# Message table of an edge network in six parts whose first turns are computed on the chip

## The chip, the cores and the metric

One core of one Trainium2 chip runs the kernel. The metric is the device time of one execution in microseconds (us). TensorE (PE), VectorE (DVE), ScalarE (ACT), GpSimd (POOL) and SyncE (SP) run side by side and meet at semaphores.

## The reference

The graph has 12,500 nodes with 128 features and 412,500 edges: 200,000 random pairs in both directions and a self loop for each node, sorted by destination. Two layers follow each other.

```python
# layer 0
agg = segment_sum(edge_weight[:, None] * x[src], dst)
x = layernorm(x + relu((x + agg) @ W1 + b1) @ W2 + b2)
# layer 1
h1 = x @ lin1_w.T
c = 0.5 * (cos(edge_weight * pi / 10) + 1)
s = softplus(edge_attr @ nn_w1.T + nn_b1) - log(2)
msg = (softplus(s @ nn_w2.T + nn_b2) - log(2)) * c[:, None] * h1[dst]
agg = segment_sum(msg, src)
out = layernorm(x + (h1 + agg) @ lin2_w.T + lin2_b)
```

Layer 0 sums over the destination, by which the edges are sorted. Layer 1 reads its rows by the destination and sums over the source, by which they are not sorted.

## The kernel before

The edges are cut into T = 403 tiles of 1024 edges (SUB = 8 columns of 128). The program has five stages: a setup, the edges of layer 0, the nodes of layer 0, the edges of layer 1 (`layer1_edges`) and the nodes of layer 1.

**Edges of layer 0.** For each tile POOL gathers eight times 128 rows of x (L432, tile `xg`), from indices that ACT copies (`gidx`, L411). DVE builds one-hot columns (`onehot`, L563), and PE multiplies the two (L475). The tiles xg, gidx and onehot have one buffer each: POOL waits for the multiplication that last read its row tile, ACT for the gathers that last read its indices. Beside this, PE computes the first layer of the edge network (L481, into two banks), ACT its softplus (L395 to L399), and DVE finishes it in `hidden(t, 0)` and `hidden(t, 1)` (L506); SP stores it (L363).

**Sorting for layer 1.** The same stage works out where each message will go. The sources fall into NB = 100 buckets of 128 nodes. The tiles are split into PARTS = 4 parts of 101, 101, 101 and 100 tiles. In each part every bucket owns whole blocks of 512 rows (floor(count/512) + 1 of them) in a table in DRAM (`sorted_messages`, two tables, each of two parts). DVE counts the sources of each bucket with `count_bucket` (L699), an operation over all columns of the part. For part 0 that is done in the setup, 100 times over 808 columns. For the part after the current one it is done once in each tile, between `hidden(t, 0)` and `hidden(t, 1)` (L589 to L592). At the start of a part `plan_part` turns the counts into row numbers, into `ends` (the last block of each bucket) and into the lists `slot_node` and `slot_row`, with small DVE operations and small matmuls (L438 to L449, L510 to L535). SP clears with zeros the last block of each bucket, one clear in each tile (L376), and two blocks at the end of each part (L382), since only the last block is partly filled.

**Edges of layer 1.** For each tile DVE makes the messages (L1248, L1257), and POOL scatters them with eight indirect DMAs to their rows (L1204). The blocks are summed in turns of TURN = 3: SP loads 3 blocks (792 KB, L1061, two buffers), DVE makes a one-hot matrix for each (`hot`, L1286), PE sums (L1132, four fp32 matmuls for a block) and DVE adds the result to `aggT` (L1297). A slot without a block is treated like the others and adds to a spare column. The first `alone` = 101 + 4 = 105 tiles run with no turn beside them. Then one turn follows each tile: turn k beside tile k + 105, for SUMMING = 298 tiles. What is left of the turns runs after the last scatter, as many pairs of turns as the chip reads in `tail`.

```python
PARTS = 4
PT = -(-T // PARTS)
SLOTS = TURN * PT
SUMMING = T - PT - BEHIND
```

Part q has the fixed slots q × 303 to q × 303 + 302, which are the turns from q × 101 on. Only the tail stops at the last block in use.

Of the kernel before, what the change touches and what calls it, by code (L numbers as in the profile page):

```python
# [33 lines left out]
PARTS = 4  # L34
PT = -(-T // PARTS)
PART_COLS = PT * SUB
TURN = 3
SLOTS = TURN * PT
PART_ROWS = SLOTS * BLOCK
TABLES = 2  # L40
TABLE_PARTS = PARTS // TABLES
TABLE_TILES = TABLE_PARTS * PT
TABROWS = TABLE_PARTS * PART_ROWS
BEHIND = 4
SUMMING = T - PT - BEHIND
PAIRS = NB + SUB
PLAN_STEPS = 9
assert SUMMING % 2 == 0 and TABLE_TILES % 2 == 0
assert PT * TE // BLOCK + NB < SLOTS and NB < PT


def edge_network_kernel(nc, x_rows, x_cols, src_cols, dst_cols, w_cols, dst_rows,
# [8 lines left out]
    with ctx:  # L61
# [3 lines left out]
        def sem(name):  # L65
            return ctx.enter_context(nc.semaphore(name))
# [9 lines left out]
        sorted_d = [nc.dram_tensor(f"sorted_messages{k}", [TABROWS + TE, RW], f32, kind="Internal").ap() for k in range(TABLES)]  # L76
# [30 lines left out]
        ends = sb("ends", [P, PARTS * PT], i32)  # L107
        tail = sb("tail", [P, 1], i32)
        slot_node = sb("slot_node", [P, PARTS * SLOTS + TURN], i32)
        slot_row = sb("slot_row", [P, PARTS * SLOTS + TURN], i32)  # L110
# [10 lines left out]
        with ExitStack() as c0:  # L121
# [9 lines left out]
            hits = sb0("hits0", [P, PART_COLS], bf16)  # L131
# [5 lines left out]
            counted0 = sem("first_part_counted")  # L137
# [12 lines left out]
            with nc.Block() as block:  # L150
# [95 lines left out]
                def _(dve):  # L246
                    dve.memset(least[:, :], 0).then_inc(cleared, 1)
                    dve.memset(most[:, :], 0).then_inc(cleared, 1)
                    dve.memset(slot_node[:, PARTS * SLOTS:], NPAD)
                    dve.memset(slot_row[:, PARTS * SLOTS:], 0)  # L250
                    dve.wait_ge(cleared, 2)

# [51 lines left out]
        with ExitStack() as c1:  # L304
# [3 lines left out]
            with ExitStack() as c2:  # L308
# [10 lines left out]
                hits = sb2("hits", [P, PART_COLS], bf16)  # L319
# [6 lines left out]
                turns_f = sb2("turns_f", [P, 2], f32)  # L326
# [15 lines left out]
                parts = [(q, q * PT, min((q + 1) * PT, T)) for q in range(PARTS)]  # L342
# [9 lines left out]
                with nc.Block() as block:  # L352
                    @block.sync
                    def _(sp):
# [13 lines left out]
                        for k in range(TABLES):  # L368
                            with sp.Fori(k * TABLE_TILES, min((k + 1) * TABLE_TILES, T)) as t:
                                sp.wait_ge(z1_set, made(t, 1))  # L370
                                sp.dma_start(attr[0:GAUSS + 1, :, :].rearrange("a h e -> a (h e)"), attr_cols[:, ds(t * TE, TE)]).then_inc(attr_in, 16)
                                store_hidden(t)
                                wait_apart(sp, ends_ready, t + 1, passed_sp)
# [605 lines left out]
def layer1_edges(nc, sem, sbuf, dst16, hid_d, h1_parts, sorted_d, dstf, rank, meta, cols, basef, base, nwin,  # L979
# [37 lines left out]
    def tail_pairs(engine):  # L1017

        return engine.value_load(tail[0:1, 0:1], min_val=1, max_val=most_pairs)
# [438 lines left out]
```

## Time and profile before

| | us |
|---|---|
| median of 3 runs (lowest, highest) | 9315.23 (9307.72, 9319.87) |
| profiled execution | 9315.85 |
| its span in the trace | 9314.2 |
| first gather of layer 0 | at 158.0 |
| last gather of layer 0 | at 4368.7 |
| first and last matmul of a turn (L1132) | at 5620.2 and 9211.2 |
| busy PE / DVE / ACT / POOL | 6033.2 / 6494.6 / 3471.8 / 6297.2 |

Times in the rows are us from the start of the span. An indirect DMA shows on POOL as the time in which it is issued; its landing is later. A line of a timeline has start, duration, engine, line of the kernel, output <- inputs, count, and in brackets the idle time of the engine before it with what ended it. "issue" is a wait for nothing that the profile shows. The trace records each fp32 matmul of a 128-column operand twice (L475: 6448 records for 3224 calls). The stages other than the two edge stages take little: the setup runs to about 155 us, the nodes of layer 0 take about 170 us, those of layer 1 about 100 us.

### The profile page before, as it was taken

How to read it: one execution, taken by the hardware profiler on the slowest of the kernel's cores; microseconds unless marked ns; L12 is line 12 of the kernel's file. 1: busy time of each engine (PE TensorE's matmuls, PEld its weight loads, DVE VectorE, ACT ScalarE, POOL GpSimd, SP SyncE). 2: the span in 40 equal slices, each digit the busy share in tenths (PEclk: the TensorE clock that was granted, in tenths of full speed). 3: DMA queues.
4: the chain of work that ended last, by engine and by line, in shares of the span. 5: the costliest groups of instructions: out<-in, count | busy, mean ns of one | idle time of the engine just before them, and what ended most of it. 6: DMA issues, size and time to landing. Idle time of an engine off the chain costs nothing. (4 is left out here: it accounts for less than half of the span.)

```text
span 9314.2 us, 204001 instructions
## 1 busy us (share of the span) xinstructions
PE 6033.2 (65%) x35189; PEld 4808.1 (52%) x35190; DVE 6494.6 (70%) x20428; ACT 3471.8 (37%) x6781; POOL 6297.2 (68%) x6541
## 2 busy tenths in 40 slices
PE   2666666666666666666655556666666666666676
PEld 1444444444444444444444446666666666666665
DVE  7777777777777776665655556777777777777655
ACT  2333333333333333333544443333333333333202
POOL 2777777777777777775277777777777777777400
PEclk8676766776767667776855557888888888888887
DMA  3444444444444444444444446666666666666554
GB/s 101 148 146 147 148 144 146 149 146 143 146 149 147 145 145 148 149 147 142 143 134 134 134 134 199 208 210 206 205 206 208 209 207 206 205 207 207 174 167 147
DMA packets 803241, 1533.30 MB, mean 165 GB/s; under 512 B 193070, under 2 KB 206820, under 8 KB 802707
## 3 DMA queue, kind: packets, MB, share of 16 engines
q1 hardware_dynamic: 593415, 1093.58, 36.2%
q0 software_dynamic: 209456, 436.16, 15.7%
q10 hardware_dynamic: 348, 3.33, 0.1%
q14 instruction: 16, 0.13, 0.0%
q8 instruction: 6, 0.10, 0.0%
HBM read 967.92 MB, written 564.58 MB: 165 GB/s over the span
## 5 line engine op out<-in xcount | busy, mean ns | idle before, releaser
L1204 POOL DMA_INDIRECT sorted_messages<-rows,sidx x3224 | 3212.4, 996 | 1154.7 <-issue 932.4
L432 POOL DMA_INDIRECT xg<-x_rows,gidx x3224 | 3043.0, 944 | 1306.8 <-issue 1020.2
L475 PE MATMUL bank<-onehot,xg 128*128 128x42 f32 x6448 | 1116.6, 326 | 1400.4 <-DMA xg<-x_rows,gidx 1386.2
L475 PEld LDWEIGHTS bank<-onehot,xg 128*128 128x128 f32 x6448 | 1004.2, 233 | 1474.0 <-DMA xg<-x_rows,gidx 1457.1
L1132 PE MATMUL bank<-hot,block_rows 128*128 128x128 f32 x9312 | 1576.2, 347 | 145.4 <-DVE hot L1286 145.1
L1132 PEld LDWEIGHTS bank<-hot,block_rows 128*128 128x128 f32 x9312 | 1530.3, 260 | 169.2 <-issue 154.0
L481 PE MATMUL bank<-attr,nn 128*128 128x512 f32 x1612 | 1453.7, 1057 | 3.0 <-DVE hid L506 3.0
L1102 PE MATMUL bank<-w_nn2T,e_hid 128*128 128x128 f32 x6448 | 1039.0, 314 | 162.2 <-DMA e_hid<-hidden 162.1
L1102 PEld LDWEIGHTS bank<-w_nn2T,e_hid 128*128 128x128 f32 x6448 | 1007.8, 226 | 245.3 <-DMA e_hid<-hidden 212.1
L1113 PE MATMUL bank<-h1w,ohT 128*128 128x128 bf16 x3224 | 349.4, 275 | 1069.6 <-DVE ohT L1233 1066.4
L1257 DVE SCALAR_TENSOR_TENSOR rows<-filt,meta,bank 128x128 f32<-128x128 f32 x3224 | 904.7, 343 | 94.7 <-DVE filt L1248 47.2
L563 DVE TENSOR_SCALAR onehot<-cols,rel,wgt 128x42 f32<-128x42 f32 x3224 | 734.8, 327 | 233.2 <-PE bank L475 230.5
L1286 DVE TENSOR_TENSOR hot<-cols,block_rows 128x512 f32<-128x512 f32 x1167 | 800.2, 686 | 118.0 <-DMA block_rows<-sorted_messages 117.5
L1113 PEld LDWEIGHTS bank<-h1w,ohT 128*128 128x128 bf16 x3224 | 266.7, 123 | 1144.4 <-issue 1144.2
L395 ACT ACTIVATE soft<-bank 128x512 f32<-128x512 f32 x808 | 474.8, 588 | 1008.5 <-PE bank L481 1004.0
L1166 ACT ACTIVATE rows<-meta 128x4 f32 (+1 forms) x806 | 167.4, 208 | 1743.0 <-DMA sorted_messages<-rows,sidx 1743.0
L1248 DVE SCALAR_TENSOR_TENSOR filt<-bank,soft 128x512 f32<-128x512 f32 x806 | 555.0, 689 | 344.7 <-issue 188.3
L1157 ACT ACTIVATE soft<-bank 128x512 f32<-128x512 f32 x806 | 481.2, 597 | 734.9 <-PE bank L1102 553.3
L411 ACT ACTIVATE gidx<-srci 128x4 int32 x806 | 165.5, 205 | 1543.2 <-DMA xg<-x_rows,gidx 1357.7
L481 PEld LDWEIGHTS bank<-attr,nn 128*128 128x128 f32 x1612 | 483.2, 329 | 422.5 <-issue 411.4
L1297 DVE TENSOR_TENSOR aggT<-aggT,bank 128x128 f32 x1164 | 328.9, 283 | 435.6 <-issue 258.9
L506 DVE SCALAR_TENSOR_TENSOR hid<-bank,soft 128x512 f32<-128x512 f32 x808 | 542.9, 682 | 4.6 <-ACT soft L399 4.6
(180 smaller groups left out, 7427.8 us busy)
## 6 DMA issues: line engine op xcount, KB each, us to landing
block_rows<-sorted_messages SPq DMA_DIRECT2D x389, 792.0 KB
hidden<-hid SPq DMA_DIRECT2D x404, 512.0 KB
e_hid<-hidden SPq DMA_DIRECT2D x403, 512.0 KB
sorted_messages<-zero SPq DMA_DIRECT2D x403, 264.0 KB
dstb<-dst SPq DMA_DIRECT2D x403, 256.0 KB
attr<-attr_cols SPq DMA_DIRECT2D x403, 204.0 KB
xg<-x_rows,gidx POOLq DMA_INDIRECT x3224, 4.2
sorted_messages<-rows,sidx POOLq DMA_INDIRECT x3224
```

The lines of the kernel that those rows point to most:

```text
L432: pool.indirect_dma_start(xg[s][:, :], None, x_rows, bass.IndirectOffsetOnAxis(ap=gidx[s // HALF][:, s % HALF:s % HALF + 1], axis=0),).the ...
L475: nc.tensor.matmul(bank[0][:, 0:WIN], xg[s][:, :], onehot[:, s, :], start=(s == 0), stop=(s == SUB - 1)).then_inc(summed, 1)
L481: nc.tensor.matmul(bank[2 + h][:, :], nn1[:, :], attr[:, h, :], start=True, stop=True).then_inc(z1_set, 1)
L506: dve.scalar_tensor_tensor(hid[:, h, :], bank[2 + h][:, :], 0.0, soft1[h][:, :], ALU.max, ALU.add).then_inc(hid_set, 1)
L563: ins = dve.tensor_scalar(onehot[:, s, :], cols[:, 0:WIN], rel[:, s:s + 1], wgt[:, ds(here + s, 1)], ALU.is_equal, ALU.mult)
L1102: ins = nc.tensor.matmul(bank[2 + h][:, s * P:s * P + P], hid[:, h, s * P:s * P + P], nn2T[:, :], start=False, stop=(s == HALF - 1))
L1113: ins = nc.tensor.matmul(bank[4 + h][:, s * P:s * P + P], ohT[:, at:at + P], h1w[:, :], start=True, stop=True)
L1132: ins = nc.tensor.matmul(sums[u][:, 0:P], block_rows[k][:, u, s, 0:D], hot[u][:, s, :], start=(s == 0), stop=(s == HALF - 1))
L1204: pool.indirect_dma_start(table, bass.IndirectOffsetOnAxis(ap=sidx[b][h][:, s:s + 1], axis=0), rows[b][h][:, s, :], None).then_inc(landed[ ...
L1248: dve.scalar_tensor_tensor(filt[h][:, :], bank[2 + h][:, :], 0.0, soft2[h][:, :], ALU.max, ALU.add).then_inc(filt_set, 1)
L1257: ins = dve.scalar_tensor_tensor(rows[b][h][:, s, 0:D], filt[h][:, part], meta[:, ds(here + (h * HALF + s), 1), 1], bank[4 + h][:, part], ...
L1286: dve.tensor_tensor(hot[u][:, :, :], cols[:, :].rearrange("p (o n) -> p o n", o=1).broadcast_to([P, HALF, P]), block_rows[k][:, u, :, D:D ...
```

## The change

The parts become six, of 45, 90, 90, 90, 44 and 44 tiles. Table 0 holds parts 0 and 1, table 1 the other four. `alone` becomes 45 + 4 = 49 and SUMMING 354. Each part counts its buckets beforehand in the part ahead of it, with 3, 2, 2, 2 and 3 counts in a tile (PER_TILE), over the first 34, 50, 50, 50 and 34 tiles of it (TILES_WITH); after these there are none in it. SP clears in the same tiles, that many blocks in each, with 34 tiles of the last part too. The tiles of a part thus run in two loops, one with and one without this work, on SP and DVE.

`plan_part` ends with five more small operations. They work out how many turns the part takes, and so the turn at which the next part starts: right behind it, but never before FIRST_TURN, the turn by which its tiles are done. The slots of the next part are written there, and `tail` is worked out from the end of the last part. The lists are first filled with empty slots in the setup (two memsets of 1783 columns). `filt` moves into the space of `wgt`.

```diff
-PARTS = 4
-PT = -(-T // PARTS)
+PART_TILES = (45, 90, 90, 90, 44, 44)
+FIRST_TILE = [sum(PART_TILES[:q]) for q in range(PARTS + 1)]
+WORST = [n * TE // BLOCK + NB for n in PART_TILES]
-SUMMING = T - PT - BEHIND
+SUMMING = T - PART_TILES[0] - BEHIND
+FIRST_TURN = [min(FIRST_TILE[q + 1] - PART_TILES[0], SUMMING + 1) for q in range(PARTS)]
...
+        FIRST_TURN[q] = LATEST_TURN[q] = SWITCH_TURN
+    LATEST_TURN.append(max(LATEST_TURN[q] + -(-WORST[q] // TURN), FIRST_TURN[q + 1] if q + 1 < PARTS else 0))
+PER_TILE = [-(-NB // n) for n in PART_TILES]
+TILES_WITH = [-(-NB // p) for p in PER_TILE]
...
-                    dve.memset(slot_node[:, PARTS * SLOTS:], NPAD)
-                    dve.memset(slot_row[:, PARTS * SLOTS:], 0)
+                    dve.memset(slot_node[:, :], NPAD).then_inc(slots_cleared, 1)
+                    dve.memset(slot_row[:, :], 0).then_inc(slots_cleared, 1)
...
+                        def tile(t, q, clears):
...
+                            for i in range(clears):
+                                clear(q, ds((t - FIRST_TILE[q]) * clears + (q * ENDS + i), 1), 1)
+                        for q, first, past_last in parts:
+                            with sp.Fori(first, first + TILES_WITH[q] - 1) as t:
+                                tile(t, q, PER_TILE[q])
+                            with sp.Fori(first + TILES_WITH[q] - 1, past_last) as t:
+                                tile(t, q, 0)
+                            for b in range(PER_TILE[q] * (TILES_WITH[q] - 1), NB):
+                                clear(q, slice(q * ENDS + b, q * ENDS + b + 1), 1)
...
+                            if q == 0:
+                                at = slice(0, SLOTS)
+                            else:
+                                dve.reg_load(slot_reg, slot_at[0:1, 0:1])
+                                at = ds(dve.snap(slot_reg, min_val=0, max_val=TURN * LATEST_TURN[q]), SLOTS)
...
+                            dve.tensor_scalar(turns_f[:, 0:1], bank[5][:, 256 + NB - 1:256 + NB], 1.0, 1.0 / TURN, ALU.add, ALU.mult).then_inc(plan, 1)
+                            dve.tensor_single_scalar(turns_f[:, 1:2], turns_f[:, 0:1], MAGIC, ALU.add).then_inc(plan, 1)
+                            dve.scalar_tensor_tensor(turns_f[:, 0:1], turns_f[:, 1:2], MAGIC, turn_at[:, :], ALU.subtract, ALU.add).then_inc(plan, 1)
+                            dve.tensor_single_scalar(turn_at[:, :], turns_f[:, 0:1], float(FIRST_TURN[q + 1] if q + 1 < PARTS else 0), ALU.max).then_inc(plan, 1)
+                            dve.tensor_single_scalar(slot_at[:, :], turn_at[:, :], float(TURN), ALU.mult).then_inc(plan, 1)
...
+                            for i in range(counts_here):
+                                at = (t - first) * counts_here + i
+                                dve.wait_ge(bucket_counts, at + COUNTED[q])
+                                count_bucket(dve, counts, bucket16, cols, hits, q + 1, at).then_inc(bucket_counts, 1)
...
-    filt = [sbuf(f"filt{h}", [P, HE], f32) for h in range(2)]
+    filt = [wgt[:, h * HE:(h + 1) * HE] for h in range(2)]
-    alone = PT + BEHIND
+    alone = PART_TILES[0] + BEHIND
-            change = TABLE_TILES // 2 - 1
+            change = SWITCH_TURN // 2 - 1
```

## Rows read from the trace of the kernel before

**Rows 1.** The page's 40 equal slices of the span, busy tenths of POOL

```profile
POOL 2777777777777777775277777777777777777400
```

**Rows 2.** Waits of POOL in the edges of layer 0: us in total, times, longest

```profile
POOL xg L432 <- issue: 879.9, 2732, 2.4
POOL xg L432 <- PE bank L475: 166.5, 283, 8.1
POOL xg L432 <- ACT gidx L411: 120.1, 201, 1.8
```

**Rows 3.** Windows of L432 within each part: length, busy (gathers), clock, DMA share, GB/s

```profile
400.00:1225.00 825.00, 600.21 (x637) 0.72 0.46 147
1229.00:2280.00 1051.00, 761.42 (x807) 0.69 0.46 147
2287.00:3330.00 1043.00, 755.17 (x800) 0.70 0.46 146
3345.00:4360.00 1015.00, 739.96 (x785) 0.71 0.47 147
```

**Rows 4.** Groups of DVE by form, then timeline of the setup's first count and its end

```profile
L699 DVE TENSOR_SCALAR_CACHE_REDUCE hits<-bucket,cols 128x808 bf16<-128x808 bf16 x302 | 316.4, 1048 | 3.5
L552 DVE TENSOR_TENSOR oha<-bank,bucket 128x800 bf16<-128x800 f32 x403 | 395.7, 982 | 0.2
...
L288 DVE TENSOR_TENSOR aggT<-wgt,aggT 128x3224 f32<-128x3224 f32 x1 | 3.5, 3518 | 0.0
...
44.44 1.05 DVE L699 TENSOR_SCALAR_CACHE_REDUCE hits<-bucket,cols 128x808 bf16<-128x808 bf16 x1
...
154.09 0.37 DVE L301 CAST basef<-base 128x403 f32<-128x403 int32 x1
```

**Rows 5.** Timeline of DVE in one tile of layer 0, with a count in it

```profile
2006.24 1.78 DVE L563 TENSOR_SCALAR onehot<-cols,rel,wgt 128x42 f32<-128x42 f32 x8 [0.81 <-PE bank L475]
...
2009.99 0.27 DVE L578 TENSOR_TENSOR bank<-bank,seen 128x100 f32<-128x100 f32 x1 [0.64 <-PE bank L465]
...
2012.61 0.68 DVE L506 SCALAR_TENSOR_TENSOR hid<-bank,soft 128x512 f32<-128x512 f32 x1
2013.21 1.04 DVE L699 TENSOR_SCALAR_CACHE_REDUCE hits<-bucket,cols 128x808 bf16<-128x808 bf16 x1
...
2014.18 0.68 DVE L506 SCALAR_TENSOR_TENSOR hid<-bank,soft 128x512 f32<-128x512 f32 x1
...
2016.62 1.85 DVE L563 TENSOR_SCALAR onehot<-cols,rel,wgt 128x42 f32<-128x42 f32 x8 [0.73 <-PE bank L475]
```

**Rows 6.** Timeline at the starts of parts 2 and 3: POOL, and two plan operations

```profile
2287.86 0.94 POOL L432 DMA_INDIRECT xg<-x_rows,gidx  x1 [6.30 <-PE bank L475]
...
3345.76 0.94 POOL L432 DMA_INDIRECT xg<-x_rows,gidx  x1 [5.73 <-PE bank L475]
...
2279.07 0.16 DVE L512 CAST bucket_rows_i<-bank 100x1 int32<-100x1 f32 x1 [5.19 <-PE bank L443]
2279.26 0.15 DVE L514 TENSOR_SCALAR bucket_blocks_i<-bucket_rows_i 100x1 int32<-100x1 int32 x1
```

**Rows 7.** One us, its store and clear under way: PE, PEld, DVE, ACT, POOL, clock, DMA, GB/s

```profile
2006.00:2007.00 1.00, 1.00 (x3) 0.48 (x3) 0.76 (x4) 0.00 (x0) 0.69 (x2) 0.50 0.95 334
```

**Rows 8.** Windows of L1204 (scatters): tiles alone, then tiles with a turn beside them

```profile
4700.00:5600.00 900.00, 683.77 (x710) 0.53 0.43 134
5800.00:8630.00 2830.00, 2172.31 (x2158) 0.83 0.65 207
```

**Rows 9.** The tail: matmuls of the turns, the drain, and the window of L1286

```profile
L1132 PE MATMUL bank<-hot,block_rows x9312: 274/300/554, 5620.2 to 9211.2; 128*128 128x128 f32 x199
...
8772.33 0.69 DVE L1286 TENSOR_TENSOR hot<-cols,block_rows 128x512 f32<-128x512 f32 x1 [19.64 <-DMA block_rows<-sorted_messages]
...
8772.30:9211.90 439.60, 184.70 (x270) 0.84 0.52 164
```

**Rows 10.** Timeline of SP at the end of the edges of layer 0

```profile
4380.73 4.91 SPq L382 DMA_DIRECT2D sorted_messages<-zero  x4
```

More of the change, by code:

```diff
@@ L341, in edge_network_kernel @@
                 blocks_cleared = sem("blocks_cleared")
-                parts = [(q, q * PT, min((q + 1) * PT, T)) for q in range(PARTS)]
+                parts = [(q, FIRST_TILE[q], FIRST_TILE[q + 1]) for q in range(PARTS)]
                 def made(k, h):
@@ L367, in _, with clear @@
                         end = sp.alloc_register("sp0_end")
[L368 to L373, printed above, removed]
-                                sp.reg_load(end, ends[0:1, ds(t, 1)])
-                                row = sp.snap(end, min_val=0, max_val=TABROWS - BLOCK)
-                                sp.dma_start(sorted_d[k][ds(row, BLOCK), :].rearrange("(p g) d -> p (g d)", p=P), zero[:, :]).then_inc(blocks_cleared, 16)
+                        def clear(q, i, blocks):
+                            sp.reg_load(end, ends[0:1, i])
+                            row = sp.snap(end, min_val=0, max_val=TABROWS - 2 * BLOCK)
+                            sp.dma_start(sorted_d[TABLE[q]][ds(row, blocks * BLOCK), :].rearrange("(k p g) d -> p k (g d)", k=blocks, p=P),
+                                         zero[:, :].rearrange("p (o e) -> p o e", o=1).broadcast_to([P, blocks, 4 * RW])).then_inc(blocks_cleared, 16)
@@ L378, in _ @@
                         for q in range(PARTS):
[L380 to L383 removed]
+                            clear(q, slice(q * ENDS + NB, q * ENDS + NB + 1), 2)
@@ L593, in _ @@
+                            with_counts = first + TILES_WITH[q] if q + 1 < PARTS else first
+                            if q + 1 < PARTS:
+                                with dve.Fori(first, with_counts) as t:
+                                    tile(t, q, first, PER_TILE[q])
+                            with dve.Fori(with_counts, past_last) as t:
+                                tile(t, q, first, 0)
                         end = jobs.number()
@@ L1215, in windows_of @@
                     sent.step(b)
-            for k in range(TABLES):
-                in_pairs(pool, k * TABLE_TILES, min((k + 1) * TABLE_TILES, T), lambda t, b: windows_of(t, b, sorted_d[k]))
+            change = FIRST_TILE[TABLE_FIRST_PART[1]]
+            for k, first, past_last in ((0, 0, change), (1, change, T)):
+                in_pairs(pool, first, past_last, lambda t, b: windows_of(t, b, sorted_d[k]))
             for b in range(2):
```

177 lines of the change are left out of this document (94 added, 83 removed).

## Prediction, made before the changed kernel was run

> **What bounds the kernel now.** I read the page first for the shape of the run. POOL is busy at 0.7 in every slice of both edge stages and at nothing else, and falls away in the last four slices [rows 1]. That is the signature of an engine that issues without pause, with a stage behind it in which it has no work. The waits of POOL in the edges of layer 0 say the same: most of its idle time is "issue", the 0.3 us after each DMA, and only 286.6 us is put down to PE or ACT [rows 2]. So the windows of its DMAs give the pace. A gather comes each 825/637 = 1.295 us in part 0, that is 10.36 us for a tile of eight; parts 1 and 2 give 10.42 and 10.43, and part 3, in which DVE counts nothing, 10.34 [rows 3]. The scatters of layer 1 give 900/710 × 8 = 10.14 us for a tile alone, and 2830/2158 × 8 = 10.49 us with a turn beside it [rows 8]. After the last scatter there is a tail that only SP, PE and DVE work on, at 439.6 us for 270 blocks, 4.88 us for a turn of three [rows 9].
>
> The span is therefore: setup, 403 tiles at POOL's pace, the nodes, 403 tiles at POOL's pace, tail, nodes. An edit is worth something if it shortens the setup or the tail, or if it changes the pace of POOL.
>
> **How many turns there are.** A bucket with c messages in a part takes floor(c/512) + 1 blocks. 101 tiles give an ordinary bucket 101 × 1024 × 0.97/97.7 = about 1030 messages, so mostly three blocks; 90 tiles give about 915, two blocks; 45 and 44 give about 450, one block. Buckets whose own nodes' self loops lie in the part have 128 more, and often one block more. Counted over the reference's own sources, the four parts take 261, 260, 260 and 252 blocks, and the six 112, 218, 212, 218, 112 and 110.
>
> Before, the last part starts at turn 303 and takes 84, so it ends at 387, and in pairs at 388. The trace has 9312 records of L1132, eight for a block (four matmuls, each recorded twice): 1164 blocks, 388 turns [rows 9]. 298 lie beside tiles, 90 in the tail. After, the parts run over turns 0 to 38, 90 to 163, 184 to 255, 270 to 343, 343 to 381 and 381 to 418. With 354 beside tiles, 64 are left, 32 pairs.
>
> **The change part by part.**
>
> *Tail.* 26 turns fewer at 4.88 us: **−127 us**. The drain ahead of it, in which the first block load waits for the last scatters to land (19.64 us), stays [rows 9]. All turns load 792 KB and do the same matmuls, so I see no reason for another price per turn; I allow 4.6 to 5.1, which is −120 to −133.
>
> *Turns beside tiles.* 56 tiles move from alone to beside a turn, at 10.49 − 10.14 = 0.35 us: **+20 us** [rows 8]. Empty slots run in windows of the same pace. The Trainium skill (SBUF — State Buffer, Who interferes with whom) says that a DVE instruction with two SBUF inputs contends with a GpSimd instruction that reads SBUF; `hot` is one, and the mean scatter is longer with turns beside it (2172.31/2158 = 1.007 us against 683.77/710 = 0.963) [rows 8]. The page gives no price for it, and the sum uses the row.
>
> *Setup.* 100 counts go from 808 to 360 columns. They run back to back: from 44.44 to 154.09 us, 1.097 us each, of which the operation itself is 1.048 [rows 4]. The slope per column comes from one operation at two sizes, (3518 − 982)/(3224 − 800) = 1.046 ns [rows 4], so each count saves 448 × 1.046 = 0.469 us: **−47 us**. If the count scaled wholly with its columns, the saving would be 0.58 us each (−58); with a flatter slope of 0.9 ns, −40. Nothing else in the setup runs that late. The two memsets of 1783 columns lie in the wait of DVE for the bias rows at its start.
>
> *Three counts in a tile, part 0.* Here 34 tiles get three counts of 720 columns where one of 808 was. From one onehot to the next DVE takes 10.38 us, with waits of 0.64 (for PE) and 0.73 (for the last gather) in it, so its own work is 9.01 us [rows 5]. One count costs 0.97 us there (2013.21 to 2014.18) [rows 5]. With 88 columns fewer it costs 0.88, and a count that must wait for the one before it 1.097 − 0.092 = 1.005. Three are 2.89, so DVE needs 9.01 + 1.92 = 10.93 us for a tile, above POOL's 10.36. DVE becomes the bound in these tiles by about 0.57, and register work for the computed count numbers may add 0.1 each. 34 × 0.6: **+20 us** (15 to 30).
>
> *Two counts in a tile.* 100 tiles get two of 720: 9.01 + 0.92 = 9.93 us, 0.4 below POOL's pace. The later `hidden(t, 1)` does no harm either, since PE takes it up only behind the last gather. 50 tiles get two of 352 (+0.13) and 34 three of 352 (+0.75): also hidden. The rest have none, and row for row that is worth at most 10.43 − 10.34 = 0.09 us each [rows 3]. **0**. If no wait of DVE could take them up, it would be 100 × 0.92 + 50 × 0.13 + 34 × 0.75 = +124, which is the other end.
>
> *Starts of parts.* At a start POOL stands for 5.73 to 6.30 us where it otherwise stands for 0.30 [rows 6], because `plan_part` lies between DVE's last tile and the next one-hot: about 5.7 us lost. There are five inner starts instead of three. Five more small operations at 0.19 us apart (2279.07 to 2279.26) [rows 6] and a register load add some 1.3 us to each. 5 × 7.0 − 3 × 5.7 = **+18 us** (+11 if the new operations were hidden, +25 if a load costs more). The first `plan_part` lies in the wait for the x_cols load.
>
> *Clears.* There are 588 single clears instead of 403, 185 more at 264 KB, two or three in a row. A store and a clear together bring the DMA to 0.95 of its time at 334 GB/s for about a microsecond or two after 2005 [rows 7], a third of the way into the tile, and SP's queue is idle again well before the next tile's last gather, which is what PE waits for. **0**. The other end is that each clear delays a gather by its own transfer, 0.27 MB / 334 GB/s = 0.81 us. At the end of the stage six instead of four double clears are issued, at 1.23 us each [rows 10]: **+3 us** with their landing.
>
> Sum: −127 + 20 − 47 + 20 + 18 + 3 = −113 us. The profiled execution took 9315.85 us (span 9314.2), as good as the median of 9315.23. So **9202 us**.
>
> **The rivals.**
>
> *The clears collide with the gathers.* Gather latency reaches POOL through gidx, which ACT writes only when four gathers have landed; POOL already waits for ACT 201 times and for PE 283 times [rows 2], so the cover is thin. Against it: the bursts fall early in the tile. At the full 0.81 us, 185 × 0.81 = +150, and the result is 9352, slower than before. It decides from 113/185 = 0.61 us for a clear. Chance 0.06 for slower by this, 0.02 for the narrow strip about no change.
>
> *DVE's waits do not take up the second count.* The tiles with two counts then run at DVE's pace, with the reads of registers between the operations. At the full price it is +124, again about no change or slightly slower; at half of it, 9264. Against it: 1.37 us of waits in the row [rows 5]. Chance 0.11 for 9240 to 9290.
>
> *A count locks POOL out.* Each count would add its time to POOL: after the change 302 × 0.96 + 202 × 0.57 = 405 us against 302 × 1.048 = 316 [rows 4], +89, so 9291. The rows speak against it: with a count in every tile the pace is 10.36 to 10.43, without 10.34, where a lock would show a full 1.05 [rows 3]. The Trainium skill (SBUF — State Buffer, Who interferes with whom) excepts the form of tensor_scalar that writes out its accumulator from the operations that can take the shared ports, and by that the trace agrees. Chance 0.02.
>
> *The turns are not packed as the code means.* If the last part started where the worst case puts it (turn 435), the tail would have (435 + 37 − 354) = 118 turns, 54 more than forecast: +264, so 9466. The arithmetic is small integers in fp32 and I see no slip. Chance 0.02.
>
> *More than forecast.* Tiles with neither clear nor count could come down towards eight gathers at 0.94 + 0.30 us [rows 6], about 10.0: 151 tiles by 0.3 is −45, so 9157. Chance 0.05.
>
> **How the numbers follow.** The forecast has 0.72: 9202, with its own terms' bounds 9180 to 9235. Its range is widened at the top for the second rival and a little at the bottom: 9170 to 9255, beyond which lie parts of the rivals that sum to less than 2 in 10. Runs of this kernel differ by 0.13% (9307.72 to 9319.87), so 0.2%, 19 us, is about what can be told. Faster: 0.72 + 0.11 + 0.02 + 0.05 = 0.90. Within: 0.02. Slower: 0.06 + 0.02 = 0.08.
>
> **What would show each step.** First gather at 111 instead of 158 us. Windows of L432 in the first 34 tiles at 10.9 to 11.1 us for a tile with DVE never waiting for PE before onehot; tiles with two counts at 10.3 to 10.45. POOL's gap at five starts of about 7 us. L1132: 418 turns, 10,032 records. L1204 at 10.14 us for 49 tiles and 10.49 for 354. L1286 at 4.88 us for each turn in a tail of some 64 turns. The prediction is wrong if the pace of two-count tiles passes 10.6 (an unhidden count or clear), or if the time for a tail turn moves: I have taken a mean over 90 turns for 64.

## The result, and the profile after

The changed kernel takes 9365.74 us (median of 5, 9352.97 to 9382.75) against 9319.87 us of the kernel before on the same chip (median of 5, 9307.72 to 9330.61): ratio 1.0053, 95% interval 1.0041 to 1.0065. It is slower by 0.5% where I had forecast 9202 us, and the range to 9255 us doesn't hold it. The profiled execution took 9352.97 us (span 9351.3), 37.1 us more than that of before.

By stage, from the first and last start of each stage's DMAs and matmuls:

| | before | after | difference | forecast |
|---|---|---|---|---|
| setup, to the first gather | 158.0 | 111.7 | −46.3 | −47 |
| gathers of layer 0, first to last | 4210.7 | 4391.4 | +180.7 | +38 |
| last gather to first scatter | 200.8 | 206.1 | +5.3 | +3 |
| scatters, first to last | 4194.2 | 4210.9 | +16.7 | +20 |
| last scatter to last matmul of a turn | 447.5 | 328.2 | −119.3 | −127 |

Everything but the second line came about nearly as forecast. The page says the same at a glance. Of POOL's 40 slices [rows 1] and the GB/s under them, after:

```profile
POOL 3666677667767776667267777777777777777710
GB/s 143 172 140 164 166 128 121 162 164 134 122 162 170 135 122 165 171 168 181 138 138 135 195 207 209 205 206 206 209 206 205 208 207 207 205 207 208 207 151 146
```

Where the last three slices of before were 4, 0 and 0, the last two are 1 and 0 now: the tail is shorter. In exchange the first half has sixes where it had sevens, mostly in the slices in which the DMAs move 160 to 180 GB/s; where they move 121 to 138, the seven is back. The first are mainly tiles with counts and clears, the others mainly tiles without.

The windows of the gathers (L459, which was L432) show it tile by tile. Columns: window and its length, busy time of POOL (gathers), granted clock, share of DMA, GB/s. Eight gathers are a tile.

```profile
140.00:500.00 360.00, 228.91 (x243) 0.70 0.54 175
530.00:635.00 105.00, 74.41 (x80) 0.69 0.39 119
660.00:1160.00 500.00, 344.09 (x365) 0.69 0.52 165
1260.00:1600.00 340.00, 249.71 (x266) 0.74 0.40 122
2600.00:3100.00 500.00, 356.23 (x378) 0.68 0.53 170
3150.00:3530.00 380.00, 274.21 (x291) 0.69 0.39 120
3550.00:3900.00 350.00, 231.32 (x245) 0.66 0.56 179
4055.00:4390.00 335.00, 237.93 (x252) 0.68 0.60 196
```

Part 0 with three counts and three clears in a tile: 360 × 8 / 243 = 11.85 us. Part 0 without them: 10.50. Part 1 with two of each: 10.96, without: 10.23. Part 3, whose two counts have 352 columns: 10.58, without: 10.45. Part 4, three of 352 columns and three clears: 11.43. Part 5, three clears and no count: 10.63. Before, every tile took 10.34 to 10.43 [rows 3]. Part 2 is as part 1 (362 gathers in 500 us, 11.05; without, 10.24).

The excess over before's pace, part by part: 34 × 1.49 + 11 × 0.14 = 52; 50 × 0.54 − 40 × 0.19 = 19; 50 × 0.62 − 40 × 0.19 = 23; 50 × 0.24 + 40 × 0.11 = 16; 34 × 1.09 = 37; 34 × 0.29 = 10. That is +157. With the starts of parts it accounts for the stage. At the five starts POOL stands for 8.89, 7.89, 7.36, 8.60 and 6.82 us (two of them here), which is 38.1 over the usual 0.3 where three starts cost about 17: +21 (forecast +18).

```profile
655.66 0.94 POOL L459 DMA_INDIRECT xg<-x_rows,gidx  x1 [8.89 <-PE bank L502]
...
4050.17 0.94 POOL L459 DMA_INDIRECT xg<-x_rows,gidx  x1 [6.82 <-PE bank L502]
```

A tile with two counts, DVE's timeline (to be laid beside [rows 5]), and SP's in the same stretch:

```profile
902.38 1.84 DVE L600 TENSOR_SCALAR onehot<-cols,rel,wgt 128x42 f32<-128x42 f32 x8
...
905.58 0.23 DVE L611 TENSOR_TENSOR pair<-bucket 128x64 f32 x1 [1.15 <-issue]
...
909.04 0.95 DVE L749 TENSOR_SCALAR_CACHE_REDUCE hits<-bucket,cols 128x720 bf16<-128x720 bf16 x1
...
910.18 0.96 DVE L749 TENSOR_SCALAR_CACHE_REDUCE hits<-bucket,cols 128x720 bf16<-128x720 bf16 x1 [0.18 <-DVE hits L749]
...
911.07 0.69 DVE L533 SCALAR_TENSOR_TENSOR hid<-bank,soft 128x512 f32<-128x512 f32 x1
...
911.80 0.98 DVE L589 TENSOR_TENSOR oha<-bank,bucket 128x800 bf16<-128x800 f32 x1
913.12 1.79 DVE L600 TENSOR_SCALAR onehot<-cols,rel,wgt 128x42 f32<-128x42 f32 x8 [0.33 <-PE bank L502]
```

```profile
911.94 0.39 SPq L378 DMA_DIRECT2D hidden<-hid  x1
913.43 1.38 SPq L388 DMA_DIRECT2D sorted_messages<-zero  x2
```

From one onehot to the next are 10.74 us, of which 0.33 is a wait for PE. The rest, 10.41, is already more than POOL's 10.36. The two counts with what lies between them take 2.03 us (909.04 to 911.07). And `pair` waits 1.15 us for "issue". What "issue" is here, the rows of the sequencers show. At the head of each tile PE, ACT, POOL and DVE each read the next tile's number of windows from `nwin` in SBUF into a register (L703), DVE its first node from `base` as well. Between `rel` and `pair` DVE executes nothing while its sequencer does that. In part 1's tiles with counts and clears (first row below) this load has a median of 598 ns and goes up to 799; in those without (second) it has 307.

```profile
L703 DVEq TENSOR_LOAD <-nwin x46: 306/598/799, 664.4 to 1156.1; - x46
...
L703 DVEq TENSOR_LOAD <-nwin x33: 301/307/320, 1269.9 to 1598.8; - x33
```

The tail and the turns are as the code means. There are 10,032 matmul records (418 turns). In the window of L1336 (DVE's `hot`, three to a turn) a turn of the tail takes 320 × 3 / 191 = 5.03 us; the drain is as before (19.73 us) [rows 9].

```profile
L1181 PE MATMUL bank<-hot,block_rows x10032: 274/325/553, 5192.3 to 9248.3; 128*128 128x128 f32 x197
```

```profile
8930.00:9250.00 320.00, 131.26 (x191) 0.83 0.49 158
```

### The profile page after: what moved, and what is told of

Read it like the earlier page. It is cut to its first block and busy times, and to the rows that moved or that the text cites. A ratio compares the mean times of both kernels' runs of the same rounds, so it can differ in the third digit from the quotient of the medians.

```text
span 9351.3 us, 207738 instructions
## 1 busy us (share of the span) xinstructions
PE 6095.0 (65%) x35927; PEld 4898.3 (52%) x35928; DVE 6620.1 (71%) x21063; ACT 3470.1 (37%) x6781; POOL 6314.6 (68%) x6541
## 5 line engine op out<-in xcount | busy, mean ns | idle before, releaser
L459 POOL DMA_INDIRECT xg<-x_rows,gidx x3224 | 3043.6, 944 | 1440.2 <-issue 945.1
L502 PE MATMUL bank<-onehot,xg 128*128 128x42 f32 x6448 | 1147.5, 328 | 1447.3 <-DMA xg<-x_rows,gidx 1433.9
L1181 PE MATMUL bank<-hot,block_rows 128*128 128x128 f32 x10032 | 1714.4, 349 | 112.9 <-DVE hot L1336 112.8
L1181 PEld LDWEIGHTS bank<-hot,block_rows 128*128 128x128 f32 x10032 | 1664.8, 262 | 134.5 <-issue 116.2
L1151 PEld LDWEIGHTS bank<-w_nn2T,e_hid 128*128 128x128 f32 x6448 | 924.0, 208 | 137.3 <-DMA e_hid<-hidden 104.4
L1151 PE MATMUL bank<-w_nn2T,e_hid 128*128 128x128 f32 x6448 | 939.9, 293 | 81.0 <-DMA e_hid<-hidden 81.0
L1307 DVE SCALAR_TENSOR_TENSOR rows<-wgt,meta,bank 128x128 f32<-128x128 f32 x3224 | 905.0, 343 | 101.4 <-DVE wgt L1298 59.7
L1336 DVE TENSOR_TENSOR hot<-cols,block_rows 128x512 f32<-128x512 f32 x1257 | 863.7, 687 | 92.9 <-DMA block_rows<-sorted_messages 92.8
L1215 ACT ACTIVATE rows<-meta 128x4 f32 x806 | 167.1, 207 | 1677.1 <-DMA sorted_messages<-rows,sidx 1677.1
L1298 DVE SCALAR_TENSOR_TENSOR wgt<-bank,soft 128x512 f32<-128x512 f32 x806 | 555.1, 689 | 266.5 <-issue 184.9
L1347 DVE TENSOR_TENSOR aggT<-aggT,bank 128x128 f32 x1254 | 355.5, 283 | 489.2 <-issue 306.3
```

The costliest lines, as they stand in the source:

```text
L459: pool.indirect_dma_start(xg[s][:, :], None, x_rows, bass.IndirectOffsetOnAxis(ap=gidx[s // HALF][:, s % HALF:s % HALF + 1], axis=0),).the ...
L502: nc.tensor.matmul(bank[0][:, 0:WIN], xg[s][:, :], onehot[:, s, :], start=(s == 0), stop=(s == SUB - 1)).then_inc(summed, 1)
L1151: ins = nc.tensor.matmul(bank[2 + h][:, s * P:s * P + P], hid[:, h, s * P:s * P + P], nn2T[:, :], start=False, stop=(s == HALF - 1))
L1181: ins = nc.tensor.matmul(sums[u][:, 0:P], block_rows[k][:, u, s, 0:D], hot[u][:, s, :], start=(s == 0), stop=(s == HALF - 1))
L1298: dve.scalar_tensor_tensor(filt[h][:, :], bank[2 + h][:, :], 0.0, soft2[h][:, :], ALU.max, ALU.add).then_inc(filt_set, 1)
L1307: ins = dve.scalar_tensor_tensor(rows[b][h][:, s, 0:D], filt[h][:, part], meta[:, ds(here + (h * HALF + s), 1), 1], bank[4 + h][:, part], ...
```

## The experiments

The kernel before was run again beside the experiments: 9345.9, 9354.7, 9357.8 and 9349.4 us, where it was 9319.9 beside the changed kernel. These chips and times differ by up to 0.4%, so each ratio is against the kernel before on the same chip, run beside it. The pace of a tile is read from windows that lie within one kind of tile and hold no start of a part. Where it is compared with [rows 3], the two traces can be of different chips; 0.4% of a tile is 0.04 us. Tiles with neither counts nor clears took 10.23 us in part 1 of the profiled changed kernel and 10.46 in the same part of a second profile of it, so a difference of a tenth is small beside that.

The question at first was which of the two, counts or clears, costs the stage its 143 us beyond the forecast. The first experiments take one away in time, the later ones only change the place.

### Counts without clears beside them

The single clears are issued together at the end of the stage. The gathers can be compared, the whole time can't, since layer 1 waits for 600 clears.

```diff
-                            for i in range(clears):
-                                clear(q, ds((t - FIRST_TILE[q]) * clears + (q * ENDS + i), 1), 1)
...
                         for q in range(PARTS):
+                            with sp.Fori(0, NB) as b:
+                                clear(q, ds(b + q * ENDS, 1), 1)
```

> All single clears are taken out of the tiles of layer 0 and issued in one row at the end of that stage, so the total is not to be compared (some 600 clears at about 0.8 us stand at the end of the stage). Read are the windows of the gathers. In the changed kernel a tile with two counts of 720 columns and two clears took 10.96 to 11.05 us, one with three and three 11.76, one with three counts of 352 and three clears 11.3. Theory A (DVE's further counts cost it): these stay within 0.15 us. Theory B (the clears' transfers delay the gathers): they fall to 10.4 or less. Theory C (counts and clears together: the counts push the store and the clears onto the last gathers): they fall most of the way, to about 10.5.

10110.42 us (one run). Windows of the gathers in part 0 with three counts, part 1 with two, part 4 with three of 352 columns:

```profile
140.00:490.00 350.00, 237.50 (x252) 0.66 0.39 112
640.00:1130.00 490.00, 352.26 (x373) 0.69 0.40 120
3500.00:3830.00 330.00, 236.93 (x251) 0.71 0.40 119
```

These are 11.11, 10.51 and 10.52 us for a tile, where the changed kernel has 11.85, 10.96 and 11.43. The stage from first to last gather takes 4286.5 us, 105 less than in the changed kernel. So two counts alone cost a tenth of a us, three of 720 columns 0.75. The clears have to do with most of the loss. For two counts that is what theory C foretold; three counts stayed above its 10.5.

### Clears without counts beside them

All 600 counts are done in the setup; nothing of the clears is altered. (A first form of it kept the counts in SBUF for the whole run, for which there is no room. This one gives their space back behind layer 0.)

```diff
                     for b in range(NB):
-                        dve.wait_ge(counted0, b)
-                        count_bucket(dve, counts, bucket16, cols, hits, 0, b).then_inc(counted0, 1)
+                    for q in range(PARTS):
+                        for b in range(NB):
+                            dve.wait_ge(counted0, q * NB + b)
+                            count_bucket(dve, counts[:, q * P:(q + 1) * P], bucket16, cols, hits, q, b).then_inc(counted0, 1)
```

> All counts of all parts are made in the setup (which grows by some 425 us, so the total is not compared), none in the tiles; two or three clears in a tile stay, with the counts gone. Theory C (only both together cost): tiles with two clears within 0.1 us of those without (10.2 to 10.45), tiles with three clears at 10.4 to 10.7. Theory B (each clear's own transfer): three clears at 11 or more, two at 10.8.

9687.59 us (one run, with a setup longer by 424 us). Windows: part 0 with three clears, part 2 with two, part 4 with three.

```profile
570.00:880.00 310.00, 219.15 (x232) 0.69 0.60 193
2000.00:2480.00 480.00, 344.21 (x365) 0.70 0.54 171
3900.00:4220.00 320.00, 222.60 (x236) 0.69 0.60 191
```

10.69, 10.52 and 10.85 us, and 4289.4 us for the stage. So clears alone cost little as well: 0.1 for two in a tile, 0.3 to 0.45 for three (against 10.4). Added to before's 10.4, two counts alone (+0.1) and two clears alone (+0.1) would give 10.6; together they give 10.96 to 11.05. Neither the theory that the clears collide nor the one that DVE's waits don't take up the count explains this by itself.

### The kernel before with one thing added in each part

The parts of before take, in turn, one more count in each tile; one more clear (to rows that nothing reads); both; two more clears in the part that has no count.

```diff
+EXTRA_COUNTS, EXTRA_CLEARS = (1, 0, 1, 0), (0, 1, 1, 2)
...
+                                for i in range(extra_clears):
+                                    sp.dma_start(extra_d[ds(t * (2 * BLOCK) + i * BLOCK, BLOCK), :]..., zero[:, :]).then_inc(blocks_cleared, 16)
...
+                                    for i in range(1 + EXTRA_COUNTS[q]):
```

> The kernel before with work added by part, nothing taken away: in part 0 a second count of 808 columns in each tile (the same bucket again), in part 1 one further clear of 264 KB into a table of its own, in part 2 both, in part 3 two further clears and no count. Paces before: 10.36, 10.42, 10.43, 10.34 us. Theory A: part 0 rises to about 11.0, part 1 and part 3 stay within 0.1, part 2 is like part 0. Theory B: part 1 rises to 10.8 or more and part 3 further, part 0 stays. Theory C: parts 0 and 1 rise by 0.1 to 0.2 each, part 2 to 11.0.

9438.83 us against 9354.68 (one run each). The windows of the four parts:

```profile
400.00:1245.00 845.00, 598.33 (x634) 0.69 0.46 143
1260.00:2310.00 1050.00, 754.43 (x799) 0.71 0.54 171
2330.00:3430.00 1100.00, 753.29 (x798) 0.68 0.52 163
3450.00:4475.00 1025.00, 740.15 (x784) 0.72 0.60 198
```

10.66, 10.51, 11.03 and 10.46 us, against 10.36, 10.42, 10.43 and 10.34 [rows 3]: +0.30, +0.09, +0.60 and +0.12. No theory had 10.66 for the second count alone (A had 11.0, C 10.5); the 11.03 of part 2 is as A and C had it. All four differences may be some 0.04 too large, since this chip is slower by 0.4%. Two more clears in a tile with no count cost 0.12 us, and one more beside one count 0.09; but one more clear on top of one more count costs 0.60 − 0.30 = 0.30. The waits of DVE in the last of these parts and in the one with both show why. Columns: us in total, times, longest; part 3 has 98 tiles and part 2 has 100.

```profile
DVE onehot L571 <- PE bank L483: 129.9, 95, 2.6
DVE pair L582 <- issue: 124.9, 98, 1.8
...
DVE pair L582 <- issue: 146.2, 99, 1.8
DVE bank L586 <- PE bank L473: 28.4, 35, 1.6
```

In both, the wait for "issue" is long, 1.27 and 1.48 us a tile, where it is 78.0/79 = 0.99 in part 0 of the kernel before. With no count that does no harm: DVE still stands 1.3 us a tile before onehot, waiting for PE. With two counts this wait is gone (0.06 us a tile), and what the register load takes longer lengthens the tile, as far as these waits show.

### Most counts ahead of the one-hot; even spreading; both

Two versions that were made to be faster. In the first, all counts of a tile but one move from between the halves of hid to the place behind `oha`, ahead of onehot. In the second the counts and clears stay in place but are spread evenly, two or three in the first tiles of a part and one or two in the rest. A third joins them.

```diff
                             dve.tensor_tensor(oha[:, :, :], ...).then_inc(oha_set, 1)
+                            for i in range(counts_here - 1):
+                                count_one(t, q, first, counts_here, i)
```

```diff
+def runs_of(q):
+    n, low = PART_TILES[q], NB // PART_TILES[q]
+    more = NB - low * n
+    return [(FIRST_TILE[q], FIRST_TILE[q] + more, low + 1, 0), (FIRST_TILE[q] + more, FIRST_TILE[q + 1], low, more * (low + 1))]
```

> Only the last count of a tile stays between the two halves of hidden; the others go ahead of the one-hot, where DVE had a wait. DVE's own work for a tile stays the same. If it is the work itself that costs (A), the pace stays at 10.96 to 11.05 for two counts and 11.76 for three, and the time within 15 us of 9366. If it is the lateness of the second half of hidden, and of the store and clears behind it (C), two counts fall to about 10.5, three to about 11, and the time by 70 us or more.

> Counts and clears spread evenly: in parts 1 to 3 two of each in the first 10 tiles and one in the other 80, in part 0 three in 10 and two in 35, in the parts of 44 three in 12 and two in 32. If the price per tile is steep only from the second one on (A or C), the excess falls from about 180 us to about 95: 9270 to 9290, faster than the kernel before. If every count or clear costs the same wherever it stands (B in its linear form), nothing changes: 9350 to 9370.

> Both remedies together: counts and clears spread evenly over a part, and all counts but one of a tile ahead of the one-hot. Alone they gave 0.9952 (moved) and 0.9961 (spread) of the kernel before. They overlap in part, since spread leaves fewer tiles with two. Expected 0.9925 to 0.995, the stage of layer 0 at about 4310 us. If moving acts by something that spreading undoes, no better than 0.995.

Moved: 9307.76 us, ratio 0.9952 (0.9935 to 0.9969). Spread: 9306.03 us, 0.9961 (0.9947 to 0.9975). Both: 9268.89 us, 0.9900 (0.9883 to 0.9918). Moved gave less than expected (two counts and two clears in a tile 10.64 us where 10.5 was expected), both together more (0.9900 where the best expected was 0.9925). Spread, tiles with one of each take 820 × 8 / 628 = 10.45. Either cure takes back nearly one per cent, and together they go further: the loss hangs on how many counts and clears meet in a tile, and on where the counts stand.

### Only the place of the counts, and the changed kernel beside it

The cleanest pair. One kernel is the changed kernel with all its counts behind `oha`, the other the changed kernel itself; same chip, same number of everything.

```diff
                             dve.tensor_tensor(oha[:, :, :], ...).then_inc(oha_set, 1)
+                            for i in range(counts_here):
+                                count_one(t, q, first, counts_here, i)
...
                             hidden(t, 0)
-                            for i in range(counts_here):
-                                at = (t - first) * counts_here + i
-                                dve.wait_ge(bucket_counts, at + COUNTED[q])
-                                count_bucket(dve, counts, bucket16, cols, hits, q + 1, at).then_inc(bucket_counts, 1)
                             hidden(t, 1)
```

> The changed kernel with nothing altered but the place of its counts: all of a tile's two or three stand ahead of the one-hot, none between the halves of hidden. Counts, clears and their tiles are as in the changed kernel. If the lateness of the second half and of the store behind it is what costs, tiles with two and two fall from 10.96 to 10.4, the level without either; tiles with three counts of 720 stay above 11, where DVE's own work is the bound; tiles with three of 352 fall from 11.4 to about 10.7; and the time is at 0.990 to 0.993 of the kernel before. If one count between the halves is harmless, it is no better than 0.995, which moving all but one gave.

> The changed kernel once more, as it is, on the chip of the run beside it, so that the paces and the ratio can be set side by side. Expected 1.003 to 1.007 of the kernel before, two and two at 10.9 to 11.1.

Counts moved: 9285.5 us, 0.9933 (0.9915 to 0.9950). Changed kernel: 9391.68 us, 1.0041 (1.0026 to 1.0056). So their place alone is worth 106 us. Part 1 with two counts and two clears (windows of L459, counts moved and then the changed kernel):

```profile
640.00:1140.00 500.00, 360.84 (x383) 0.73 0.55 173
```

```profile
660.00:1160.00 500.00, 341.21 (x362) 0.68 0.52 163
```

10.44 us against 11.05. The three-count tiles of part 0 have 11.25 against 11.72, those of part 4 10.80 against 11.43. DVE's waits in these two windows, counts moved first:

```profile
DVE pair L619 <- issue: 41.4, 48, 0.9
DVE bank L623 <- PE bank L492: 13.6, 25, 1.6
```

```profile
DVE pair L611 <- issue: 58.2, 46, 1.7
DVE bank L615 <- PE bank L492: 20.6, 25, 1.5
...
DVE onehot L600 <- PE bank L502: 5.8, 11, 1.2
```

Over 47.9 and 45.25 tiles, the wait for "issue" is 0.86 against 1.29 us, that for PE's counts 0.28 against 0.46, onehot's 0 against 0.13. These three differ by 0.43 + 0.18 + 0.13 = 0.74, which covers the 0.61 between the tiles. Without clears the counts took 10.51 between the halves of hid, so their old place alone costs little: it costs where the clears are beside it. And the load of `nwin` by DVE's sequencer in the two:

```profile
L707 DVEq TENSOR_LOAD <-nwin x48: 300/307/434, 643.1 to 1131.5; - x48
```

```profile
L703 DVEq TENSOR_LOAD <-nwin x46: 302/560/793, 660.5 to 1157.2; - x46
```

It is at rest where the counts are moved, though the same clears go out. The timelines say why. In the changed kernel's tile shown above, the store goes out behind `hidden(t, 1)`, the clears behind it at 913.43, and DVE's two register loads come at 915.1 and 915.5, right behind the second clear; the second of them took 0.69 us. Between the store and the loads DVE has little but `oha` and onehot. With the counts moved they lie between the two as well: the store goes out at 908.30, the clears at 909.91, and the loads follow at 913.0 and 913.4 behind the counts and onehot. They are 3.1 us behind the first clear's issue, where it was 1.7.

```profile
908.30 0.39 SPq L378 DMA_DIRECT2D hidden<-hid  x1
909.91 1.33 SPq L388 DMA_DIRECT2D sorted_messages<-zero  x2
```

It isn't the traffic itself that makes the load long. The first row is the stretch from 912.9 to 913.3 (PE, PEld, DVE, ACT, POOL, clock, DMA, GB/s): the DMA engines are at 0.95, at 364 GB/s. The second is DVE's load in it, at 307 ns.

```profile
912.90:913.30 0.40, 0.40 (x2) 0.15 (x1) 0.19 (x2) 0.37 (x2) 0.40 (x1) 0.78 0.95 364
```

```profile
L707 DVEq TENSOR_LOAD <-nwin x1: 307/307/307, 913.0 to 913.0; - x1
```

Counted over the part 1 window with the counts moved, 33 of 96 loads began with the DMA engines 90% busy or more, and their median is 308 ns. What sorts DVE's loads of `nwin` and `base` is the time since the last clear was issued. In the edges of layer 0 of the changed kernel, 259 of the 480 loads within 2 us behind a clear's issue took over 400 ns, and none of the 324 others. With the counts moved it is 103 of 159, and 1 of the 640 others. In the kernel before it was 149 of 443 already. Where there are three clears in a tile (part 3 of the kernel before with additions), 9 of the 78 loads that come later took over 400 ns too.

The paces are as expected for tiles with two counts and two clears (10.4), and a tenth above it for three counts of 352 columns (10.7).

### Only the place of the clears

The counts stay between the halves of hid; SP issues the clears behind the attr load, ahead of the store.

```diff
-                            store_hidden(t)
                             if clears:
                                 wait_apart(sp, ends_ready, q + 1, passed_sp)
                             for i in range(clears):
                                 clear(q, ds((t - FIRST_TILE[q]) * clears + (q * ENDS + i), 1), 1)
+                            store_hidden(t)
```

> The changed kernel, with the clears of a tile issued ahead of the store of the hidden layer and right behind the load of attr, instead of behind the store. Same transfers, same counts. If the place of the burst against the tile's last gathers matters (C), the paces move by 0.3 us or more in some direction: lower, 10.5 to 10.7 for two and two, if the clears now run ahead of the last gathers; higher if they run over them. The time is then off 9366 by 30 us or more. If only the amount matters (B) or only DVE's work (A), it stays within 15 us of the changed kernel.

9489.42 us, 1.0139 (1.0121 to 1.0157): slower by another per cent. Window of part 1's tiles with two of each, DVE's waits in it, and POOL's:

```profile
660.00:1190.00 530.00, 350.75 (x371) 0.67 0.51 158
```

```profile
DVE bank L615 <- PE bank L492: 46.7, 45, 1.6
DVE pair L611 <- issue: 45.6, 46, 1.0
```

```profile
POOL xg L459 <- ACT gidx L438: 49.7, 41, 2.1
```

11.43 us for a tile. Here the register load is at rest (median 307 ns), 7.8 us behind the last clear's issue, and the wait for "issue" is 0.98. In its place DVE waits 1.01 us a tile for PE's counts, and POOL 1.07 for ACT's indices (0.65 in the changed kernel, 0.33 with the counts moved), which ACT writes only when gathers have landed. The clears, out at 905.82, now fall on other work. That they delay the loop that runs through gathers, ACT and PE fits these waits, but is argued. This run shows that two clears beside the same counts cost 0.9 us a tile at this place (10.51 without clears) and 0.5 at that of the changed kernel. It also shows that the register load is not the only thing they can hit.

### The best of them

Spread evenly, and all counts ahead of onehot: the two edits above together.

> As the run before, but no count at all stays between the two halves of hidden. Theory C (the lateness of the second half and of the store behind it): the one count of the 80-tile stretches no longer delays the store by 0.97 us either, so no slower than the run before and up to 20 us faster. If what helps is only that DVE's wait ahead of the one-hot gets filled, then it is 0 to 15 us slower, since three counts (3 us) overfill that wait.

9252.0 us (9248.63 to 9262.66) against 9357.83, ratio 0.9890 (0.9872 to 0.9908). It beats both kernels. The stage takes 4277.8 us, 114 less than in the changed kernel's profile. Tiles with two of each take 340 × 8 / 262 = 10.38 us, and tiles with one of each 10.52 (part 1), so by then fewer counts and clears in a tile are no gain that these windows show.

## Why the prediction was wrong

**The step that failed** is the pair of terms put at 0, under "Two counts in a tile" and under "Clears". Tiles of parts 1 to 3 with two of each cost 50 × (0.54 + 0.62 + 0.24) = 70 us where I had 0; part 4, which I had also put at 0, 37; part 5, clears alone, 10. Part 0, with its +20, cost 52. Tiles with neither gave back 11 (in the second profile of the changed kernel, at 10.46, they gave back nothing). That is 138 us too much; with the tail's 8, the starts' 3 and some single us elsewhere it is the 151 us between 9202 and the profiled 9352.97, within what windows can tell. The number of clears was off too: there are 600 single ones, 197 more than before, and not 588 and 185. In the sum that changed nothing, since they were put at 0; the rival's +150 would have been +160.

Each was costed against a cover of its own, and it was the same cover: DVE's slack in a tile. The account of DVE, in us a tile, from the waits in the windows (its work is the pace less its waits; "itself" is the 0.2 us between dependent operations; the changed kernel is the one run beside the version with the counts moved):

| | pace | work | itself | issue | waits for PE |
|---|---|---|---|---|---|
| before, part 0 (1 count, 1 clear) | 10.36 | 8.00 | 0.19 | 1.06 | 1.11 |
| changed, part 1 (2, 2) | 11.05 | 8.81 | 0.36 | 1.29 | 0.58 |
| counts moved, part 1 (2, 2) | 10.44 | 8.87 | 0.36 | 0.92 | 0.29 |
| clears late, part 1 (2, 0) | 10.51 | 8.88 | 0.37 | 0.95 | 0.31 |
| clears first, part 1 (2, 2) | 11.43 | 8.87 | 0.37 | 0.99 | 1.20 |
| counts moved, part 0 (3, 3) | 11.25 | 9.70 | 0.56 | 0.99 | 0 |

1. *The size of DVE's tile.* I had 9.93 us for two counts. Without any wait for PE it is 8.81 + 0.36 + 1.29 = 10.46, over POOL's 10.36. Of the 0.53 that I missed, 0.25 is that the one tile that I read [rows 5] was shorter than the mean of part 0 (9.01 against 9.25). The rest is a second count at 1.0 with its wait for the first in place of 0.92, and 0.2 of the register load.
2. *The waits of DVE as slack.* I took 1.37 us of waits [rows 5] as free to fill. But with two counts 0.58 us a tile stay in the changed kernel, most of them in front of `bank`, whose sums PE makes from DVE's own `oha`: a wait for another engine that waits for this one. With the counts moved 0.29 stay. They are no fixed amount, since with three counts moved nothing is left of them (rows below, of part 0). What keeps them there with two counts was not taken apart.
3. *The clears.* "A third of the way into the tile" was read for the gathers, from a tile with one count [rows 7]. What counts here is how far behind the clears DVE's register loads come. From the store's issue to the load of `nwin` it is 3.2 us in the median in part 0 of the kernel before (one count), 4.2 in its part 3 (none) and 2.8 in the changed kernel's part 1, mainly since the second count has used up DVE's wait before onehot, which lay between the two. And there are two clears in a row behind the store. So the load is 0.22 us behind the last clear's issue where it was 1.52. With the counts moved, which then lie in between, it is 2.19. I had asked what the clears do to the gathers only. That rival ("the clears collide with the gathers") was half right: with the counts as they are, the sequencer's load suffers, by 0.25 to 0.3 us a tile in the median, and the gathers do only when the clears are issued earlier. The 0.81 us for each clear was reached nowhere. The rival "DVE's waits do not take up the second count" was right on where the bound goes and of about the right price (up to +124). But with the clears out of the way two counts cost a tenth of a us.
4. *Three counts.* Forecast 10.93 us a tile. Without clears 11.11, with the counts moved 11.25, as changed 11.85 and 11.72. DVE is the bound, as said: without clears and with the counts moved it waits for no other engine at all. The size was off by 0.2 to 0.3 for the counts (one count follows another at 1.14 us in the row above, 909.04 to 910.18, where I had 1.005) and by 0.5 to 0.7 for the clears.
5. *A count locks POOL out*: no. The same two counts without clears give 10.51.

DVE's waits in part 0 with the counts moved, 31.1 tiles, all that there are:

```profile
DVE pair L619 <- issue: 30.8, 31, 1.0
DVE hits L753 <- DVE hits L753: 11.3, 62, 0.2
DVE rank L632 <- DVE count L629: 6.1, 32, 0.2
```

**What came as forecast.** Setup: −46.3 (−47). The count of 360 columns takes 587 ns and they follow each other at 0.63 us, as the slope of 1.046 ns a column said. Starts of parts: +21 (+18). Turns: 418, 10,032 records, to the record. Scatters: +16.7 (+20); a tile with a turn beside it 10.49 us, as in [rows 8]. Clears at the end of the stage: six take 7.29 us where four took 4.91 [rows 10], and the gap grew by 5.3 (+3).

**The tail** gave 119.3 instead of 127, just short of the 120 to 133 that I had allowed: a turn takes 5.03 us where it took 4.88. The mean over 90 turns didn't quite hold for 64, which I had named as a weak point; 64 × 0.15 = 9.6 is about the difference.

**What stays open.** That DVE's load of a register is long shortly behind a clear's issue, and at rest when moved away from it, is shown; by what the issue does this is not. How the slow loads, and PE's own (median 444 ns in the changed kernel, 303 with the counts moved), share the remaining 0.3 us a tile with the later matmuls of the edge network was not taken apart. The median time from a gather's issue to its landing does not sort the cases: in part 1 it is 5.1 us in the slow changed kernel (11.05) and 5.0 in the version with late clears (10.51). So I don't name it as the cause. Why tiles with neither counts nor clears take 10.23 us in one profile and 10.46 in another is open too. The counts moved and no clears beside them was not tried. Nor was a version without any clears.

## What to carry to other kernels

Two edits that are each free because something covers them may lean on the same cover: sum all that an engine does in the new iteration, its sequencer's loads and its waits on itself included, and compare that sum with the pace. Work that fills a wait also draws together what stood before and behind it, so a burst of DMAs must be looked at in its new distance to all that follows. When an engine is near the bound, try added work on the other side of a store's producer: here that alone, with the same work, turned +0.4% into −0.7%, and spread evenly as well −1.1%.

## What the runs showed of the hardware that was not expected

DVE's load of one register from SBUF takes 0.30 us and stretches to a median of 0.56 to 0.68 us, up to 1.02, shortly behind the issue of clears on SP's queue. This was shown above for part 1 of the changed kernel; the row is of part 3 of the kernel before with additions, with three clears and no count in a tile:

```profile
L663 DVEq TENSOR_LOAD <-nwin x98: 302/592/1021, 3455.3 to 4469.4; - x98
```

With two counts and no clears in the tile it is 307 ns, so the counts don't do it. Nor do busy DMA engines alone: at 364 GB/s, 3.1 us behind the first clear, it took 307 ns as well. The engine's operations themselves are not stretched: L589 takes 0.98 us at 901.48, and at 911.80 beside the store. The Trainium skill (SBUF — State Buffer, Who interferes with whom) says that a DMA never contends with a compute engine; for the operations of DVE the trace agrees, but the engine still loses the time, by its sequencer. The Trainium skill (DMA: Bandwidth & Descriptors, Latency and other measured facts) gives about 600 ns as the floor of a tensor load. Here the undisturbed load is half of that, and about 600 ns is what DVE's takes right behind a clear's issue.

Two clears of 264 KB in a tile with two counts cost between nothing that can be told (10.44 us a tile, the counts moved) and about one us a tile (11.43, the clears moved), by where in the tile they and the counts stand.
